# A sandwich of two attention and two feed-forward layers on one Trainium2 core: the first attention's output part and the local layers' preparation merged into one part

## The reference, cut to what matters

```python
x = L0_attn_resid                                             # (4, 512, 128)
x = x + _layernorm(_L0_attn_ref(_layernorm(x), ...))          # causal attention, 32 heads
x = x + _layernorm(_L0_ffn_ref(_layernorm(x), ...))           # two local layers: window attention, feed-forward
x = x + _layernorm(_L1_attn_ref(_layernorm(x), ...))          # relative attention
x = x + _layernorm(_L1_ffn_ref(_layernorm(x), ...))           # gated feed-forward

def _layernorm(x, axis=-1, eps=1e-05):
    m = jnp.mean(x, axis=axis, keepdims=True)
    v = jnp.var(x, axis=axis, keepdims=True)
    return (x - m) / jnp.sqrt(v + eps)

# the end of _L0_attn_ref: pattern @ values, then the output product
z = jnp.einsum('bhqk,bkhr->bqhr', pattern, v_g)               # 32 heads of 8 values = 256
out = jnp.einsum('bqhd,hdm->bqm', z, W_O)                     # 256 -> 128
```

## Time and profile before

| | |
|---|---|
| three runs | 1796.22, 1798.31, 1805.46 us; median 1798.31 |
| the profiled execution | 1811.3 us, with a span of 1809.5 us |
| PE, DVE, ACT, POOL busy in the span | 84%, 70%, 61%, 24% |
| mean granted TensorE clock | 0.922 of full |

### The profile page before, as it was taken

The page is one execution under the profiler, slowest core; times in us unless marked ns, Lnnn a source line. Parts: engine busy times, 40 slices in busy tenths (PEclk is TensorE's granted clock), DMA queues, the critical chain, the costliest instruction groups (busy, mean ns, idle before and its releaser), DMA issues. The chain is left out here.

```text
span 1809.5 us, 34115 instructions
## 1 busy us (share of the span) xinstructions
PE 1515.1 (84%) x11044; PEld 941.3 (52%) x11044; DVE 1259.5 (70%) x3805; ACT 1111.8 (61%) x2617; POOL 442.8 (24%) x433
## 2 busy tenths in 40 slices
PE   4699888999899852788888888569999999999955
PEld 2265555556555532466666666435555555554434
DVE  4477777777777656788788887555777777777543
ACT  1267766677677710566767666227887887887321
POOL 1333333333333204444454444110000000000010
PEclk9699999999999966899999999868999999999777
DMA  1677777787777512111011100019999998999200
GB/s 43 171 187 183 187 187 188 187 195 190 180 190 191 144 59 94 32 25 29 16 28 29 24 22 15 26 55 329 327 324 315 325 328 293 327 323 308 100 14 24
DMA packets 152702, 281.09 MB, mean 155 GB/s; under 512 B 25824, under 2 KB 29008, under 8 KB 152400
## 3 DMA queue, kind: packets, MB, share of 16 engines
q1 hardware_dynamic: 152528, 278.91, 53.4%
HBM read 147.93 MB, written 121.37 MB: 149 GB/s over the span
## 5 line engine op out<-in xcount | busy, mean ns | idle before, releaser
L519 ACT ACTIVATE a_Pm<-a_Pm,a_nm 128x272 f32<-128x272 f32 (+3 forms) x512 | 266.6, 570 | 170.7 <-DVE a_nm L441 170.5
L441 DVE CUSTOM_DVE_ANT_0 a_Pm<-ps,a_mask 128x272 f32<-128x272 f32 (+3 forms) x512 | 237.6, 502 | 95.5 <-PE ps L358 93.9
L1672 DVE CUSTOM_DVE_ANT_0 r_Sx<-ps,r_Sx 128x512 f32<-128x512 f32 x256 | 166.7, 689 | 150.6 <-PE ps L1553 150.5
L1622 ACT COPY r_BD<-ps 128x320 f32<-128x320 f32 x512 | 192.6, 425 | 85.2 <-PE ps L1543 81.8
L1543 PE MATMUL ps<-r_R,r_qv 32*128 32x320 f32 x1024 | 224.6, 501 | 6.2 <-DVE r_qv L1662 5.5
L1553 PE MATMUL ps<-r_K,r_qu 32*128 32x256 f32 x1024 | 224.8, 437 | 3.0 <-DVE r_nb L1672 2.8
L358 PE MATMUL ps<-a_Kst,a_Qst 128*128 128x272 f32 (+4 forms) x640 | 200.9, 410 | 17.7 <-DMA a_Kst<-bounce 17.3
L1629 ACT ACTIVATE r_Sx<-r_Sx,r_nb 128x512 f32<-128x512 f32 x256 | 182.7, 715 | 29.9 <-DVE r_nb L1672 23.4
L358 PEld LDWEIGHTS ps<-a_Kst,a_Qst 128*128 128x128 f32 x640 | 113.6, 193 | 149.9 <-issue 61.8
L1563 PE MATMUL ps<-m_ident,r_Sx 128*128 128x128 f32 x1024 | 172.0, 292 | 0.5 <-DVE r_PT L1681 0.5
L373 PE MATMUL ps<-m_ident,a_Pm 128*128 128x128 f32 x1280 | 170.7, 278 | 1.4 <-ACT a_Pm L519 0.7
(11 more groups left out here) (201 smaller groups left out, 2725.5 us busy)
## 6 DMA issues: line engine op xcount, KB each, us to landing
spill<-r_BD SPq DMA_DIRECT2D x128, 640.0 KB, 4.4
r_Sx<-spill SPq DMA_DIRECT2D x128, 512.0 KB, 5.3
a_Kst<-bounce SPq DMA_DIRECT2D x128, 264.0 KB, 5.0
a_Qst<-bounce SPq DMA_DIRECT2D x128, 256.0 KB, 4.5
bounce<-a_kh SPq DMA_DIRECT2D x32, 264.0 KB, 3.5
bounce<-a_kl SPq DMA_DIRECT2D x32, 264.0 KB, 4.1
bounce<-a_qh SPq DMA_DIRECT2D x32, 256.0 KB, 5.7
bounce<-a_ql SPq DMA_DIRECT2D x32, 256.0 KB, 6.2
```

The source lines that it names most:

```text
L441: nc.vector.tensor_tensor_reduce(out=Pm[:, u % 2, qt, 0:w], in0=S[:, S_of[qt]:S_of[qt] + w], in1=mask[:, N + AV - w:N + AV], scale=-SCALE, ...
L519: nc.scalar.activation(row, row, ACT.Exp, scale=-1.0, bias=nm[:, u % 2, qt:qt + 1]).then_inc(exp_done, 1)
L1622: nc.scalar.copy(BD[:, m % BUFS, j, HW * half:HW * half + HW], ps[:, BDB[k % 3], 0:HW]).then_inc(bd_ev, 1)
L1672: nc.vector.tensor_tensor_reduce(out=row, in0=ps[:, AC + n % 2, :], in1=row, scale=-SCALE, scalar=-BIG, op0=ALU.add, op1=ALU.min, accum_ou ...
```

## The change

It makes one part of the two, in a new function `outputs_and_inputs`, which is called inside `local_layers`; the barrier between them goes. The sums are loaded as 128 partitions (4 batches of 32 heads) and inverted by one reciprocal; the selector is repeated for each batch, and spread b reads the rows of its batch. Spreads use two pairs of PSUM banks. The weights `wo` are loaded behind the first z, and z has one semaphore for each batch. POOL clears only what has to be clear, forms the rotary tables, and takes eight powers, one for each batch and norm. The norms are applied on ACT, as Identity with scale 1/deviation and bias -mean/deviation; the bias comes from a small new DVE instruction (`shift`). DVE's order is written out by hand, with the two norms of different batches interleaved.

```diff
-    a["a_sel"] = np.repeat(np.eye(AH, dtype=np.float32), AR, axis=1).reshape(AH, 2, P)
+    a["a_sel"] = np.tile(np.repeat(np.eye(AH, dtype=np.float32), AR, axis=1).reshape(AH, 2, P), (B, 1, 1))
...
+            outputs_and_inputs(nc, Store(nc, ctx0, "o"), X, zd, sd, ps, c, d, t)
...
+        @block.sync
+        def _(sp):
+            sp.dma_start(sums[:], sd.rearrange("b h n -> (b h) n")).then_inc(s_in, 16)
+            sp.dma_start(sel[:], d["a_sel"]).then_inc(w_in, 16)
+            sp.dma_start(z[:, 0], zd[0].rearrange("(j p) n -> p j n", p=P)).then_inc(z_in[0], 16)
+            sp.dma_start(wo[:], d["a_wo"]).then_inc(w_in, 16)
+            for b in range(1, B):
+                sp.dma_start(z[:, b], zd[b].rearrange("(j p) n -> p j n", p=P)).then_inc(z_in[b], 16)
...
+        @block.tensor
+        def _(pe):
+            def spread(b):
+                rows = slice(AH * b, AH * b + AH)
+                for j in range(2):
+                    if b >= 2:
+                        pe.wait_ge(z_done, 2 * (b - 2) + j + 1)
+                    nc.tensor.matmul(ps[:, 2 * (b % 2) + j, :], sel[rows, j, :], sums[rows, :], start=True, stop=True)\
+                        .then_inc(r_ready, 1)
+
+            def out_product(b):
+                pe.wait_ge(z_done, 2 * b + 2)
+                if b >= 2:
+                    pe.wait_ge(yn_done, NT * (b - 1))
...
+            pe.wait_ge(w_in, 32)
+            pe.wait_ge(r_done, 1)
+            spread(0)
+            spread(1)
+            for b in range(B):
+                out_product(b)
+                if b + 2 < B:
+                    spread(b + 2)
...
+            def table(l, cs):
+                pool.wait_ge(sc_in, 32)
+                for k in range(2):
+                    row = sc[:, l, cs, k, :].rearrange("p (o e) -> p o e", o=1).to_broadcast([P, NT, FD])
+                    nc.gpsimd.tensor_tensor(t["tab"][:, l, cs, k, :, :], base[:, cs, k, :, :], row, ALU.mult).then_inc(tabbed, 1)
...
+            def normalise_y(b):
+                act.wait_ge(y_shift, b + 1)
+                if b >= 2:
+                    act.wait_ge(x_done, b - 1)
+                for n in range(NT):
+                    nc.scalar.activation(yn[:, b % 2, n, :], ps[:, Y + b % 2, P * n:P * n + P], ACT.Identity,
+                                         scale=rstd[:, 0, b, n:n + 1], bias=shift[:, 0, b, n:n + 1]).then_inc(yn_done, 1)
...
+            def shift_y(b):
+                v.wait_ge(y_pow, b + 1)
+                nc.vector.scalar_tensor_tensor(shift[:, 0, b, :], mv[:, 0, b, :, 0], -1.0, rstd[:, 0, b, :],
+                                               ALU.mult, ALU.mult).then_inc(y_shift, 1)
...
+            def residual(b):
+                v.wait_ge(yn_done, NT * (b + 1))
+                xs = X[:, NT * b:NT * b + NT, :]
+                nc.vector.tensor_tensor(xs, xs, yn[:, b % 2], ALU.add).then_inc(x_done, 1)
...
+            v.wait_ge(s_in, 16)
+            nc.vector.reciprocal(sums[:], sums[:]).then_inc(r_done, 1)
+            scale(0)
+            scale(1)
+            moments_y(0)
+            scale(2)
+            shift_y(0)
+            moments_y(1)
+            residual(0)
+            moments_x(0)
+            shift_y(1)
+            scale(3)
+            shift_x(0)
+            moments_y(2)
+            residual(1)
+            moments_x(1)
+            shift_y(2)
+            shift_x(1)
+            moments_y(3)
+            residual(2)
+            moments_x(2)
+            shift_y(3)
+            shift_x(2)
+            residual(3)
+            moments_x(3)
+            shift_x(3)
...
-        output_and_residual(nc, X, zd, sd, ps, c, d)
-        local_layers(nc, X, ps, c, d)
+        local_layers(nc, X, zd, sd, ps, c, d)
```

More of the change, by code:

```diff
@@ L580, in arrays_of @@
     return a
[L583 to L659, removed]
@@ L699, with local_layers @@
 FE = FD + 1
-def local_layers(nc, X, ps, c, d):
+def local_layers(nc, X, zd, sd, ps, c, d):
     with ExitStack() as ctx:
@@ L714, in local_layers @@
         with ExitStack() as ctx0:
[L715 to L719, removed]
-            rstd = s0.sb("rstd", [P, TT])
-            names = w_in, sc_in, filled, tabbed, stats, var_, pow_, xb_done = s0.sems(
-                *"w_in sc_in filled tabbed stats var pow xb_done".split())
[L723 to L727, removed]
-                    for name in ("wqkv", "wo", "w1", "w2", "b1", "lgb", "band"):
-                        sp.dma_start(t[name][:], d["f_" + name]).then_inc(w_in, 16)
-                    sp.wait_ge(w_in, 7 * 16)
-                @block.gpsimd
-                def _(pool):
-                    for k, name in enumerate(("kT", "hT", "Vs", "none")):
-                        nc.gpsimd.memset(t[name][:], 0.0).then_inc(filled, 1)
-                    nc.gpsimd.memset(t["Vb"][:, :, :, FD:FE], 1.0).then_inc(filled, 1)
-                    pool.wait_ge(filled, 5)
-                    nc.gpsimd.memset(t["HT"][ONE:P, :, HC - 1, :], 1.0).then_inc(filled, 1)
-                    pool.wait_ge(filled, 6)
-                    pool.wait_ge(var_, 1)
-                    nc.gpsimd.tensor_tensor(rstd[:], mv[:, :, 1], c["mhalf"][:, 0:TT], ALU.pow).then_inc(pow_, 1)
-                @block.vector
-                def _(v):
-                    for n in range(TT):
-                        nc.vector.bn_stats(st[:, n, :], X[:, n, :]).then_inc(stats, 1)
-                    v.wait_ge(stats, TT)
-                    for n in range(TT):
-                        nc.vector.bn_aggr(mv[:, n, :], st[:, n, :]).then_inc(stats, 1)
-                    v.wait_ge(stats, 2 * TT)
-                    nc.vector.tensor_scalar(mv[:, :, 1], mv[:, :, 1], EPS, None, ALU.add).then_inc(var_, 1)
-                    v.wait_ge(sc_in, 32)
-                    for l in range(FL):
-                        for cs in range(2):
-                            for n in range(NT):
-                                nc.vector.tensor_tensor(t["tab"][:, l, cs, :, n, :], base[:, cs, :, n, :], sc[:, l, cs, :, :],
-                                                        ALU.mult).then_inc(tabbed, 1)
-                    v.wait_ge(pow_, 1)
-                    for n in range(TT):
-                        nc.vector.tensor_scalar(t["xb"][:, n, :], X[:, n, :], mv[:, n, 0:1], rstd[:, n:n + 1],
-                                                ALU.subtract, ALU.mult).then_inc(xb_done, 1)
-                    v.wait_ge(xb_done, TT)
-                    v.wait_ge(tabbed, FL * 2 * NT)
```

103 lines of the change are left out of this document (102 added, 1 removed).

## The result

Four runs of the changed kernel took 1770.60, 1773.42, 1773.42 and 1775.38 us, median **1773.42**. The kernel before, with one more run than the prediction had, stood at 1801.88 (1796.22 to 1811.27). The ratio is 0.9837, with a 95% interval of 0.9807 to 0.9867: 28.5 us, or 1.6%, faster. The prediction said 1774.5, in a range of 1766 to 1782, which holds the result. But it had worked out 23.8 us where 28.5 came, and its median came out right partly because the kernel before then stood 3.6 us lower, at 1798.31. The profiled execution took 1773.42 us, with a span 37.9 us shorter than before, and this has to be taken apart first.

The account below looks back on a forecast made before the run. Bound: an engine-to-engine chain between two barriers. DVE's last 15.65 us from 680.9 end at 696.5; with 0.92 the items start at 697.4, not 721.2: 23.8 us less, off the 1798.3 median, giving 1774.5; range 1766 to 1782.

Parts of the forecast that it names:

- The bound: Output part and preparation, between barriers: an engine-to-engine chain of some 70 us; each microsecond saved there is one of the kernel.
- The start: Chain's beginning: one reciprocal of 3.28 us, ended at 657.6; base weights `wo` in by 655.7, ahead of it.
- At the half clock one of their four halves passes in 1.72 us: Spreads 0 and 1 on PE, back to back: 1.72 us per half, so product 0 starts at 664.6.
- the overlap: PE's neighbouring spreads, on different array rows, run together: 1769 instead of 1771 us, within a rival of chance 0.20.
- I let it rise at 678: PE's clock comes to full only at 678, after the second product, as in the old part.
- the rival of the early clock: PE's clock comes up early, as products and spreads are closer together: 1771 us, or 1769 if spreads overlap; chance 0.20.
- DVE's tail: From 680.9 DVE is waited for: moments, additions, shifts, waits and ACT's last application sum to 15.65 us, ending at 696.5.
- DVE held by POOL: DVE additions and epsilons wait for POOL's powers and tables: costs 3.3 us, saving 20.5, time 1778; chance 0.16.
- Costed at nothing: Table products in POOL's pauses (a pair 1.3 to 2.6 us), ACT's other applications, SP's loads, items' half-clock start: no cost.
- POOL as the bound: Powers queue behind slow table products on POOL: saving gone at 5.7 us per product, 1809 at 7.0; chance 0.01.

Follow-up runs that it names:

- the second: The changed kernel again, unedited, with six runs: 1776.36 us, ratio 0.9843 to the kernel before; its profile's part took 46.1 us.
- without the tables: The changed kernel with POOL's eight table products left out and the tables filled with ones at the start: part 43.3 us, kernel 1771.93 us.
- the busy start: The changed kernel with four 128x512 products on PE ahead of the first spread: 1768.25 us; again with six runs, 1769.82 us, ratio 0.9819 to the kernel before.
- the attempt to change it: The changed kernel with four 128x512 products ahead of the first spread and fifteen behind the last output product: part 38.5 us, kernel 1768.29 us.
- the small memsets: The kernel before, with POOL clearing only the parts of four buffers that have to be clear: part 61.4 us, kernel 1797.45 us.

## Why the prediction was right, and where it wasn't

**The bound.** That a microsecond of the part is one of the kernel fits the runs, but only roughly. The part is 29.3 us shorter than before in the first profile and 23.8 in the second, the medians 28.5 and 28.0. That 29.3 and 28.5 lie so close is partly luck: what lies outside the part took between 1726.5 and 1741.4 us over the fourteen profiles.

**The start.** The reciprocal of 128x512 took 3.35 us (3.28 forecast, 4.34 as the other end). `wo` was not in at 655.7 in the old count but half a us after the reciprocal's end. Over the twelve profiles with the new start `wo` landed between 0.6 us before and 0.6 behind the reciprocal's end, so the two are about a tie, and the 1.9 us between them weren't there. I had worked them out from a mean rate of 260 GB/s and from 0.95 MB; the selector has grown fourfold, and the loads come to 1.05 MB. PE started 6.6 us after the sums' issue, with 6.35 forecast.

**PE.** This is the step that failed: "At the half clock one of their four halves passes in 1.72 us", one after another. They passed in pairs, 3.79 us for both spreads instead of 6.9. I had kept the overlap for a rival, at 2 us; the runs show about 3 for it. The other term, "I let it rise at 678", is no constant of the kernel. Counted from the first spread, my rise lay at some 20 us. Three profiles with the same list on PE show 7.6, 16 (without the tables) and 24. In the first the part took 40.7, and the rival of the early clock (27.3, or 29 with overlap) describes it. In the third it took 46.1, the forecast's 697.4 - 651.2 to within 0.1, but by luck: the overlap that I had left out and a clock that came up some 4 us later than I had it cancel. What the part took in the runs that were only timed is not shown; their medians, 28.5 and 28.0 less, are nearer to the rival's 29 than to my 23.8.

**DVE's tail.** Forecast 680.9 to 697.4, 16.5 us from the moments of product 2 to the items. It measured 682.54 - 665.82 = 16.7 in the first profile and 16.7 in the second as well. The waits of 0.95, 0.95, 1.15 and 0.5 were 1.06, 1.06, 1.12 and 0.35; four applications on ACT took 1.5 and 1.65 (1.5 taken).

**DVE held by POOL.** The rival had the mechanism half right and its price too high (3.3). It is the shifts that are held by table products, for 0.7 us in all. The additions that I had feared for keep 0.68 beside a power; there it is POOL that takes 1.38 instead of 1.01, with slack to spare. What decides is which of the two starts first, as the busy start shows, where one power began 0.07 us ahead of the addition:

```profile
661.46 1.01 POOL L715 TENSOR_TENSOR o_rstd<-o_mv,m_mhalf 128x4 f32<-128x4 f32 x1 [0.83 <-DVE o_mv L793]
661.53 0.69 DVE L816 TENSOR_TENSOR m_X<-m_X,o_yn 128x512 f32<-128x512 f32 x1 [0.16 <-ACT o_yn L760]
```

This power took 1.01 and the addition 0.69, and it is the same in the three other profiles in which the power came first. A power that starts 0.17 behind the addition takes 1.38, 0.24 behind it 1.31; a shift 0.07 behind a table product takes 0.68, and 0.42 behind it 0.33. So the later one is held, until about the end of the earlier one. The prediction also says that no row of the kernel before shows this for two inputs. One might: the first table product on DVE (L756), two SBUF inputs, took 3.26 us and its sisters 0.28, and it too ended at 707.08, with POOL's memset; but it stood behind the held epsilon, so the trace does not tell which of the two it waited for. The Trainium skill (GPSIMD Engine Reference, "Key points") names two SBUF inputs as a case of contention; the trace agrees for both instructions, but the loser is now one engine, now the other, and the applications that took 1.86 us instead of 1.11 have only one SBUF tensor as input.

**Costed at nothing.** The tables (1.41 a pair, between the bounds) and ACT's other applications were covered. The items' start at the half clock was right, and stayed so in spite of the attempt to change it. What I had not named: the early load of the items' weights, without which the small memsets would have given 1.9 us of their gain back to that load.

**POOL as the bound.** Nothing of it was seen. A table product took 0.7 us, an eighth of the 5.7 from which it decides.

## What to carry to other kernels

Where several short chains go from engine to engine, write their orders so that one chain's step fills the other's wait: here this gave 11.7 of 29.3 us, and putting an operation on a free engine 3. When a chain starts behind an idle PE, products over all rows in the idle time can bring the clock up: they did in all four profiles here, and the part took 38.0, 38.2 and 38.5 us where the changed kernel's took 40.7 and 46.1. One profile of a kernel is no measure of a part of this length. When a part is merged with its predecessor, look at the loads too, since they may be what is late next.

## What the runs showed of the hardware that was not expected

Two matrix products of 32 rows each, on different rows of the array and into different banks, passed beside each other although another product of the first rows stood between them in the list: 3.79 us for eight records against 3.78 for four. The time until the granted clock rises varied from 7.6 to over 27 us in nine profiles in which PE began with work on 32 rows and was nearly always busy (two of them had a pause of 3.6 us), and from 7.6 to 24 in two profiles of the same kernel; with work on 128 rows it rose within 3 to 6 us of the start of that work in all five profiles. A VectorE instruction of four columns took 0.68 us instead of 0.16 when it started 0.07 us behind a two-input product on GpSimd; a power on GpSimd took 1.38 instead of 1.01 when it started 0.17 behind a two-input VectorE addition, and 1.01 when it started 0.07 ahead of it.
